# Two-layer graph network on one core: the tensor product's sum over 16 operand planes, without the VectorE folds

## The reference, cut to what matters

```python
R = relu(abs_distances[:, None] @ w1 + b1) @ w2 + b2     # 384 radial numbers per edge
Y = spherical_harmonics(rel_vec)
Fj = features[src]                                        # gather of 32 numbers per edge
for i, (mo, lo) in enumerate(RS):                         # RS = [(8, 0), (8, 1)]
    for j, (mi, li) in enumerate(RS):
        for k, lf in enumerate(range(abs(lo - li), lo + li + 1)):
            acc = acc + NORM[i] * einsum('euv,ef,evi,ofi->euo', Rb[..., k], Yf, Fb, C)
msg = concatenate(msg_blocks, axis=-1)
out = out.at[dst].add(msg)
```

## Time and profile before

| | |
|---|---|
| median of the runs | 9813.86 us |
| profiled execution, own time | 9813.76 us |
| its span, first to last instruction | 9812.0 us |
| POOL busy | 7567.6 us (77%) |
| DVE busy | 5195.8 us (53%) |
| PE busy | 3551.0 us (36%) |
| ACT busy | 1902.4 us (19%) |
| mean granted TensorE clock | 0.693 |

### The profile page before, as it was taken

One profiled execution on the slowest core, in us unless ns is written; L12 is line 12 of the kernel. 1 busy time (PEld: TensorE's weight loads), 2 busy tenths in 40 slices (PEclk: granted clock), 3 DMA queues, 4 the chain that ended last, 5 costly groups with the idle time before them and its releaser, 6 DMA issues. The chain is left out here.

```text
span 9812.0 us, 72045 instructions
## 1 busy us (share of the span) xinstructions
PE 3551.0 (36%) x20406; PEld 2961.2 (30%) x20406; DVE 5195.8 (53%) x6829; ACT 1902.4 (19%) x1824; POOL 7567.6 (77%) x6677
## 2 busy tenths in 40 slices
PE   1000000000000000000027777777777777777773
PEld 0000000000000000000016666666666666666662
DVE  3233333333333333333337878787777778777773
ACT  0121111121111112111102222222222222222220
POOL 6777777777777777777677777777777777777773
PEclk8555555555555555555558999998888899899986
DMA  6122222222222222222123333333333333333331
GB/s 266 39 57 52 52 52 56 51 56 53 52 52 52 56 51 58 52 52 52 44 58 76 84 85 81 87 80 86 80 80 83 82 83 83 84 80 82 83 80 32
DMA packets 417129, 692.59 MB, mean 71 GB/s; under 512 B 170350, under 2 KB 247902, under 8 KB 405070
## 3 DMA queue, kind: packets, MB, share of 16 engines
q1 hardware_dynamic: 174376, 356.79, 13.4%
q0 software_dynamic: 213216, 166.16, 10.6%
q10 hardware_dynamic: 29382, 168.33, 4.2%
HBM read 345.81 MB, written 190.98 MB: 55 GB/s over the span
## 5 line engine op out<-in xcount | busy, mean ns | idle before, releaser
L901 POOL DMA_INDIRECT feat<-scratch_h,src x3132 | 3606.2, 1151 | 973.4 <-issue 954.6
L476 POOL DMA_INDIRECT kv<-scratch_kv,src_i x3132 | 3552.4, 1134 | 968.3 <-issue 954.6
L1175 DVE TENSOR_TENSOR prod<-psR,ops 128x384 f32<-128x384 f32 (+1 forms) x3132 | 1917.3, 681 | 53.5 <-issue 43.2
L927 PE MATMUL psS<-prod,ident 128*128 128x192 f32 x11136 | 1895.4, 326 | 0.0
L927 PEld LDWEIGHTS psS<-prod,ident 128*128 128x128 f32 x11136 | 1825.6, 190 | 34.9 <-issue 1.5
L692 PE MATMUL psA<-ident,tail 128*36 128x128 f32 x3 | 0.8, 414 | 4691.0 <-DVEq L717 4691.0
L581 DVE TENSOR_TENSOR qk<-qrun,kv 128x1728 f32<-128x1728 f32 x58 | 184.9, 3188 | 2557.1 <-DMA kv<-scratch_kv,src_i 2557.1
L692 PEld LDWEIGHTS psA<-ident,tail 128*36 128x36 f32 x3 | 0.3, 129 | 4691.6 <-DVEq L717 4691.6
L916 PE MATMUL psR<-whigh,stack 128*128 128x384 f16 x3132 | 1069.5, 342 | 238.5 <-DVE prod L1175 221.4
L917 PE MATMUL psR<-wlow,capped 128*128 128x384 f16 x3132 | 1060.0, 339 | 0.0
L930 PE MATMUL psS<-prod,ident 128*128 128x192 f32 x2784 | 604.7, 355 | 888.4 <-DVE prod L1183 888.4
(11 more groups left out here) (246 smaller groups left out, 3789.1 us busy)
## 6 DMA issues: line engine op xcount, KB each, us to landing
units<-in_wT SPq DMA_DIRECT2D x348, 288.0 KB
scratch_state<-out ACTq DMA_DIRECT2D x58, 1080.0 KB
scratch_qexp<-zeros ACTq DMA_DIRECT2D x32, 1566.0 KB, 43.8
kv<-scratch_kv,src_i POOLq DMA_INDIRECT x3132
qin<-scratch_qexp SPq DMA_DIRECT2D x58, 864.0 KB, 4.5
feat<-scratch_h,src POOLq DMA_INDIRECT x3132
stack<-high SPq DMA_DIRECT2D x348, 144.0 KB
stack<-low SPq DMA_DIRECT2D x348, 144.0 KB
```

What stands on the lines that cost most here:

```text
L476: nc.gpsimd.indirect_dma_start(kv[b][:, t, :], None, a["kv"], bass.IndirectOffsetOnAxis(ap=src_i[b][:, t:t + 1].bitcast(U32), axis=0)).the ...
L901: nc.gpsimd.indirect_dma_start(feat[b][:, t, :], None, a["h2"], bass.IndirectOffsetOnAxis(ap=src_i[b][:, t:t + 1].bitcast(U32), axis=0)).t ...
L927: nc.tensor.matmul(psS[:, r, 0:GC].rearrange("p (t c) -> p t c", c=COLS), ident[:, :], prod[r][:, :, j, :], start=(n == 0), stop=False)
L1175: v.tensor_tensor(to[:, :, :, lo:lo + n], psR[:, g % 2, :, frm:frm + n * JC].rearrange("p t (j u) -> p t j u", j=JC), ops[b][:, ts, x * JC ...
```

## The change

The folds go. TensorE sums all 16 planes itself, in one run of matmuls, after the wait for all six product instructions; the semaphore `prod_ready` goes with the folds. Nothing else is touched: the tiles, the other semaphores and the order of the other work stay.

```diff
-FOLDS = (3, 2, 3) * PACKS
...
                     pe.wait_ge(sum_free, q + 1)
                     pe.wait_ge(prod_done, q * 6 + 12)
-                    order = [j for j in range(FOLDS[s], JC) if not JC // 2 <= j < JC // 2 + FOLDS[s]]
-                    for n, j in enumerate(order):
-                        nc.tensor.matmul(psS[:, r, 0:GC].rearrange("p (t c) -> p t c", c=COLS), ident[:, :], prod[r][:, :, j, :], start=(n == 0), stop=False)
-                    pe.wait_ge(prod_ready, q + 1)
-                    for j in range(FOLDS[s]):
-                        last_mm = nc.tensor.matmul(psS[:, r, 0:GC].rearrange("p (t c) -> p t c", c=COLS), ident[:, :], prod[r][:, :, j, :], start=False, stop=(j == FOLDS[s] - 1))
+                    for j in range(JC):
+                        last_mm = nc.tensor.matmul(psS[:, r, 0:GC].rearrange("p (t c) -> p t c", c=COLS), ident[:, :], prod[r][:, :, j, :], start=(j == 0), stop=(j == JC - 1))
                     last_mm.then_inc(sum_ready, 1)
...
-                def fold(b, c, s):
-
-                    r, q = (b * SPC + s) % 2, c * SPC + s
-                    vec.wait_ge(prod_done, q * 6 + 12)
-                    v.tensor_tensor(prod[r][:, :, 0:FOLDS[s], :], prod[r][:, :, 0:FOLDS[s], :], prod[r][:, :, JC // 2:JC // 2 + FOLDS[s], :], ALU.add).then_inc(prod_ready, 1)
...
                             if s % 3 == 2 and not (last and b == 1):
                                 split(i, (b + 1) * PACKS + s // 3)
-                            fold(b, c, s)
```

More of the change, by code:

```diff
@@ L821, in tensor_product @@
         units_ready, high_ready, split_done, parts_seen = sem("units_ready"), sem("high_ready"), sem("split_done"), sem("parts_seen")
-        radial_ready, prod_done, prod_ready, sum_ready, sum_free = (sem(n) for n in (
-            "radial_ready", "prod_done", "prod_ready", "sum_ready", "sum_free"))
+        radial_ready, prod_done, sum_ready, sum_free = (sem(n) for n in (
+            "radial_ready", "prod_done", "sum_ready", "sum_free"))
         ops_copied, turned_ready, turned_copied, ops_free, flags_ready, red_free, scanned, run_copied = (sem(n) for n in (
```

## The result

The changed kernel takes 9848.57 us (9846.18 to 9853.53, 6 runs), the kernel before 9809.78 us beside it; the ratio is 1.0041 (95% interval 1.0028 to 1.0054). The forecast was 9878 us, slower, with a range of 9755 to 9990.

The account below looks back on a forecast made before the run. POOL's gathers were taken to set the pace, 78.6 us a chunk, some held up by VectorE instructions with two SBUF inputs. 9813.76 us plus 57 for gathers and 7 for the tail gave 9878 us, range 9755 to 9990.

Parts of the forecast that it names:

- (1): TensorE: summing all 16 planes makes steps 7.15 us but stays hidden behind the gathers; cost 0 before the last gather.
- (2): Tail after the last gather: ten steps of 7.15 us and a last of 5.2, +7.4 us in all.
- (3): VectorE: the 522 folds' 357.8 us go, worth 0 by themselves since VectorE is not on the path.
- (4): Gathers held up: without folds they meet SBUF stretches at other places; +1.0 us a chunk, +57 us in all.
- step 6: Two instructions of line 1145: gathers meet the stretch at 0.12 instead of 0.70 us; +0.6 us a chunk.
- step 8: Lines 1158 and 1134: wait falls from 2.43 to 2.1 us, -0.3 us a chunk.
- after the landing: Lines 1145 and 1134 after the gathers land: waits stay as before.
- steps 3, 4: Lines 1199, 1203, 1212: start at 1199 moves from 0.7 to 0.5 us, near 0 at the scans; +0.2 us a chunk.
- Rival A: Gathers keep their places and folds' port time is given back: faster, 9773 or 9689 us; chance 0.25.
- B: Rival: gathers have no fixed place and holds even out, 9832 us, or folds never held any, 9821; chance 0.13.
- C: Rival: gathers in steps 6 and 2 also lose to the next instruction, +194 us, 10015 us; chance 0.10.
- D: Rival: TensorE becomes the bound if its clock stays at the lower level throughout, +2900 us; chance 0.02.

Follow-up runs that it names:

- e12: Changed kernel plus a one-input row sum of the fold's length at the fold's place, into an unused tile; 9792.14 us, ratio 0.9919 to the kernel before.
- e11: Changed kernel plus one-input row sums before SBUF stretches: 140 elements in steps 4, 6, 7, 8, 620 in step 2; 9624.98 us, ratio 0.9739 to the kernel before.
- e1: Changed kernel with TensorE leaving planes 0 to 2 (or 0 to 1) out of the sum; 11421 us beside 11932, with TensorE standing still between matmuls.
- e6: Changed kernel plus one-input row sums of 48 elements between products and SBUF stretch in steps 4, 6, 7, 8; 11523 us, ratio 0.9925 to the kernel before.
- e7: Changed kernel plus one-input row sums of 48 elements in steps 4, 6, 7, 8 and 516 in step 2; between 11104 and 11561 us, no ratio recorded.
- e5: Changed kernel plus 192-element memsets ahead of the SBUF stretches of steps 4, 6, 7, 8; 9866.88 us, ratio 1.0033 to the kernel before.
- e4: Changed kernel plus 192-element memsets ahead of the SBUF stretches of steps 4, 6, 7, 8; 11809 us beside 11932, with TensorE standing still between matmuls.
- e10: Changed kernel plus one-input row sums of 140 elements in steps 4, 6, 7, 8 and 620 in step 2; 12561 us, ratio 1.050, TensorE's instructions 2 to 3 us apart.

## Why the prediction was right, step by step

The sum had +57 us in the gathers and +7 in the tail; measured +39 and +8 (and -8 in the attention's gathers).

The tail's evacuations in the changed kernel, on ScalarE:

```profile
9649.67 0.42 ACT L1013 ACTIVATE red<-psS,scales 128x192 f32<-128x192 f32 x1 [6.73 <-PE psS L925]
9656.82 0.42 ACT L1013 ACTIVATE red<-psS,scales 128x192 f32<-128x192 f32 x1 [6.73 <-PE psS L925]
...
9690.62 0.42 ACT L1013 ACTIVATE red<-psS,scales 128x192 f32<-128x192 f32 x1 [4.78 <-PE psS L925]
```

(1) TensorE hidden: right. These lie 7.15 us apart, as forecast, the last 5.20 behind the one before it (9685.42), and the cover held: VectorE waits 17.3 us a chunk for gathers (1003.5 / 58), and POOL's gaps are 954.2 us as before. (2) Tail: right, +8.0 for +7.4. (3) VectorE's 357.8 us worth nothing by themselves: right, and e12, which puts nearly all of them back, is faster. (4) The place on the grid: right in kind. Over the 56 chunks with gathers beside these steps the median start was 0.110 us into step 6's stretch, 0.088 in step 7 and 0.117 in step 8, where 0.12 was forecast; 0.63 in step 2 and 0.48 in step 3, for 0.63 and 0.5.

The sizes: by how much gathers took longer than 0.947 us, summed by the place that they met (us over the stage):

```
place                  before  after   diff  forecast    e12
after the landing          47     64    +17        0      77
step 6                     98    125    +27      +34      91
step 7                     61     72    +11      +11      39
step 8                    138     81    -58      -19      96
steps 1, 2                 86     90     +4      +17      79
steps 3, 4                209    254    +45      +11     221
```

The differences add up to +46; the rest to the measured +39.5 is that the gathers that nothing held had a median of 0.944 us, for 0.947 before.

Two terms were mis-sized most, with opposite signs. Step 8: 2.1 us a chunk was forecast, 1.4 measured. In 37 chunks the stretch lay where it was forecast, and there the gather lost to the instruction behind line 1153 only 18 times, where the forecast went by 41 of 41. In 12 others `products` had waited 0.6 to 0.9 us for TensorE, and the gather met the stretch 0.36 to 0.72 us in; in 7 it started within 0.05 us of the stretch's start and went through. Steps 3 and 4: the first scan was forecast a toss-up; the gather started 0.077 us into it, the unlucky side, 1.71 us instead of 1.12. The first line above was costed at nothing, "as before": but 26 of 56 gathers went through there before and 10 of 56 after. What sets the place at the landing no run shows. That these errors, -39 us at step 8 against +34 and +17, nearly cancelled in the sum was luck; the direction was not, since the places came as forecast.

Rival A (port time given back) fell by its own condition, a start above 0.5 us in steps 6 to 8. Its effect exists: step 8's waits fell by 58 us; the other places took back more. B, that places even out, had the nearer number, +18 us where +64 was forecast and +39 measured, but its mechanism is refuted by the medians above and by e11. C, that POOL loses more often, did not come: all 56 gathers in step 6 got through behind the first instruction, and step 8's lost less often than before. In e1, though, 5 of 29 lost in step 6, from the same start. D did not come: POOL showed no new wait.

What stays open: when a held gather loses to the next instruction. At line 1156 of the kernel before it lost 37 of 52 times with the same start, to within 0.05 us; at 1158, 0.9 us in, it won 15 of 15 times before and lost 55 of 56 in e12.

## What to carry to other kernels

Where one engine's fixed cadence sets the pace and another can hold it up, ask not how much time the other takes but where in its instructions each beat falls; removing work on one engine, or lengthening it on another, moves every later beat. Here 358 us of work removed, with 452 us of further planes on TensorE, cost 39 us, and 86 us of idle-looking work put in the right place saved 253. A filler for such a shift must not itself bring the hold back: with a memset in the row sum's place nothing was gained.

## What the runs showed of the hardware

- In all runs, a gather that started up to 0.03 us into a two-input VectorE instruction behind `products` went through (0.94 to 0.95 us), and from 0.045 us on each was held until 0.82 us after an instruction's end; in between both occur. Behind a row sum of 48 elements, in step 6, 41 of 42 were held from 0.00 us on (e6, e7).
- A memset of 192 elements with a two-input instruction right behind it: all 203 gathers that began 0.00 to 0.06 us into it were held to the end of that instruction or later, in e5. Where that instruction came over 1.0 us later, three took 0.94 us (e4). With a row sum of 140 elements at this place none of 197 was held (e11).
- For long times TensorE's matmul records can come 2 to 3 us apart (e1, e10), with no wait that the profile names; the same kernel on the same chip ran free of it in e11. The cause was not found.
